# A four-layer graph network on one core: four buffers for the gathered rows instead of three

## What is computed

```python
def _genconv(h, edge_attr, src, dst, w1, b1, g1, bb1, w2, b2, t):
    msg = relu(h[src] + edge_attr) + 1e-07          # h[src]: one row per edge
    m = msg * t
    ex = exp(m - segment_max(m, dst)[dst])
    alpha = ex / (segment_sum(ex, dst)[dst] + 1e-16)
    out = h + segment_sum(msg * alpha, dst)
    z = relu(_layernorm(out @ w1 + b1, g1, bb1))
    return z @ w2 + b2
h = x @ enc_node_w + enc_node_b
e = edge_attr @ enc_edge_w + enc_edge_b
h = _genconv(h, e, ...)                             # layer 0
for i in range(1, 4):                               # layers 1 to 3
    h = h + _genconv(relu(_layernorm(h, ...)), e, ...)
return layernorm(x + relu(_layernorm(h, ...)))
```

## Time and profile before

| | us |
|---|---|
| median of 3 runs | 4429.86 |
| the three runs | 4434.78, 4423.26, 4429.86 |
| span of the profiled execution | 4412.7 |

### The profile page before, as it was taken

The page is one execution under the profiler, slowest core; times in us unless marked ns, Lnnn a source line. Parts: engine busy times, 40 slices in busy tenths (PEclk is TensorE's granted clock), DMA queues, the critical chain, the costliest instruction groups (busy, mean ns, idle before and its releaser), DMA issues.

```text
span 4412.7 us, 44760 instructions
## 1 busy us (share of the span) xinstructions
PE 2914.6 (66%) x16648; PEld 1382.9 (31%) x16648; DVE 2824.3 (64%) x2795; ACT 1741.2 (39%) x2192; POOL 2517.9 (57%) x2621
## 2 busy tenths in 40 slices
PE   3667677775437776777435777777742777777764
PEld 2223233332313333333222333333331333333333
DVE  6467678778436665666753666665763565666675
ACT  3356555545223333333432333333432333433343
POOL 6565656564366665666445666665627565655642
PEclk6778788877568888888656888887855787888875
DMA  6677778877237777777534777777734677777761
GB/s 153 162 219 204 215 195 222 219 198 174 59 100 204 204 204 192 204 204 204 133 81 115 204 204 204 205 205 201 191 76 104 160 199 199 204 202 190 211 153 40
DMA packets 1041338, 774.25 MB, mean 175 GB/s; under 512 B 914394, under 2 KB 935391, under 8 KB 1017504
## 3 DMA queue, kind: packets, MB, share of 16 engines
q1 hardware_dynamic: 934256, 446.17, 42.9%
q10 hardware_dynamic: 22048, 226.63, 14.0%
q0 software_dynamic: 84816, 98.59, 9.9%
HBM read 478.68 MB, written 292.44 MB: 175 GB/s over the span
## 4 chain that ended last, share of the span: by engine, by line
PE 41%; issue 23%; DVE 11%; ACT 10%; another core or an unknown queue 10%; POOL 4%; DMA 1%; SPq 0%; ACTq 0%; POOLq 0%; DVEq 0%
PE X L537 32%; PE X L520 5%; POOL gath L479 4%; DVE decay L885 3%; PE X L547 2%; DVE state_all L916 2%; ACT msg L647 2%; DVE X L890 1%; ACT shared L676 1%; ACT X L649 1%; ACT decay L659 1%; ACT X L664 1%; DVE state_all L900 1%; ACT decay L637 1%
## 5 line engine op out<-in xcount | busy, mean ns | idle before, releaser
L479 POOL DMA_INDIRECT gath<-z_table,idx x2488 | 2396.0, 963 | 1606.0 <-issue 750.5
L537 PE MATMUL X<-one_hot,z_parts 128*64 128x512 fp8e5 x13800 | 2103.0, 427 | 840.8 <-issue 773.1
L537 PEld LDWEIGHTS X<-one_hot,z_parts 128*64 128x64 bf16 x13800 | 939.4, 120 | 2071.2 <-issue 1542.8
L883 DVE TENSOR_TENSOR decay<-decay,top 128x1 f32<-128x1 f32 x216 | 34.2, 158 | 1358.5 <-ACT X L649 1179.6
L647 ACT ACTIVATE msg<-X,edge_bias 128x1024 f32<-128x1024 f32 (+2 forms) x216 | 228.2, 1057 | 1622.5 <-remote 1080.3
L520 PE MATMUL X<-attr,enc_edge 128*128 128x512 f32 x824 | 469.3, 688 | 221.9 <-issue 115.8
L659 ACT ACTIVATE decay<-X 128x1024 f32<-128x1024 f32 (+2 forms) x216 | 209.3, 969 | 791.7 <-DVE X L890 556.1
L871 DVE STREAM_TRANSPOSE rows_all<-state_all 128x1024 f32<-128x1024 f32 (+3 forms) x432 | 505.9, 1171 | 7.5
L885 DVE TENSOR_TENSOR_SCAN decay<-X,decay 128x1023 f32<-128x1023 f32 (+2 forms) x216 | 477.2, 2209 | 7.7
L900 DVE TENSOR_TENSOR_SCAN state_all<-decay,state_all,X 128x1024 f32<-128x1024 f32 (+2 forms) x216 | 468.2, 2167 | 20.0 <-ACT X L664 16.0
L916 DVE TENSOR_TENSOR_SCAN state_all<-decay,state_all,X 128x1024 f32<-128x1024 f32 (+2 forms) x216 | 468.0, 2167 | 0.0
(11 more groups left out here) (155 smaller groups left out, 1182.3 us busy)
## 6 DMA issues: line engine op xcount, KB each, us to landing
rows_table<-rows_all SPq DMA_DIRECT2D x784, 256.0 KB
one_hot<-one_hot_dram ACTq DMA_DIRECT2D x69, 1920.0 KB
attr<-attr_t SPq DMA_DIRECT2D x196, 512.0 KB
one_hot<-one_hot_dram ACTq DMA_DIRECT2D x69, 1280.0 KB
one_hot_dram<-one_hot SPq DMA_DIRECT2D x23, 1920.0 KB
gath<-z_table,idx POOLq DMA_INDIRECT x2488
one_hot_dram<-one_hot SPq DMA_DIRECT2D x23, 1280.0 KB
keep<-keep_dram SPq DMA_DIRECT2D x192, 128.0 KB
```

Of the source, the lines that this page charges most:

```text
L479: pool.indirect_dma_start(out=gath[s][:, n * F:(n + 1) * F], out_offset=None, in_=z_table, in_offset=bass.IndirectOffsetOnAxis(ap=idx[:, c ...
L537: last = nc.tensor.matmul(x[h * F:(h + 1) * F, BANK:CH], z_parts[:, i * GB + k, third, :], one_hot[:, i, k, h * BANK:(h + 1) * BANK], star ...
```

## The change

`gath` has four buffers and four semaphores instead of three; the other buffers keep three. POOL waits before chunk g for `x_ready` of chunk g - 4. The totals that PE waits for are counted per buffer of four. No instruction is added or taken away on PE, DVE, ACT or SP, and none changes its place: in POOL's row of instructions the wait for `x_ready` of each chunk is for one chunk earlier, and the first in layer 0 stands before chunk 4 instead of chunk 3.

```diff
 SLOTS = 3
+GSLOTS = 4
...
-    GATHERS_UP_TO.append((GATHERS_UP_TO[_g - SLOTS] if _g >= SLOTS else 0) + HALVES * (gathered_tiles(_g // NCH, _c) - first_tile(_c)))
+    GATHERS_UP_TO.append((GATHERS_UP_TO[_g - GSLOTS] if _g >= GSLOTS else 0) + HALVES * (gathered_tiles(_g // NCH, _c) - first_tile(_c)))
...
-        gath = slots("gath", SLOTS, [P, KT * HALVES * F])
+        gath = slots("gath", GSLOTS, [P, KT * HALVES * F])
...
-        attr_landed, gathered, stored = sems("attr_landed", SLOTS), sems("gathered", SLOTS), sems("stored", 2)
+        attr_landed, gathered, stored = sems("attr_landed", SLOTS), sems("gathered", GSLOTS), sems("stored", 2)
...
-                    s = g % SLOTS
-                    if g >= SLOTS:
-                        pool.wait_ge(x_ready, g - SLOTS + 1)
+                    s = g % GSLOTS
+                    if g >= GSLOTS:
+                        pool.wait_ge(x_ready, g - GSLOTS + 1)
...
             def add_rows(layer, c):
                 g = layer * NCH + c
-                s = g % SLOTS
+                s = g % GSLOTS
                 pe.wait_ge(gathered[s], 16 * GATHERS_UP_TO[g])
```

## The result

The changed kernel takes 4612.80 us (median of 4 runs, 4605.57 to 4632.76), the kernel before 4432.32 (4 runs, 4423.26 to 4436.77): ratio 1.041, interval 1.038 to 1.045. Forecast were 4510 us, range 4350 to 4640. The sign and the range held; the rise is 180 us instead of 84. The profiled execution has a span of 4603.6 us, 190.9 more than the one before.

A forecast was written before the change was run, and what follows sets the result against it. The prediction took PE's slow completions during POOL's runs of gathers, until they land, to set each section's length. Terms +40 + 66 - 22 + 0 gave +84 us on the 4429.9 us median, rounded to 4510 us; range 4350 to 4640.

The forecast's parts named there:

- the term of layer 0: Layer 0, where POOL also waits for ACT's key counts: taken as 0, bounds -45 to +80 us.
- What bounds it: PE's completions turn slow some microseconds into a run of gathers and come free when it has landed; mean pair 36.3 us.
- flip of the phase: Steady pairs: long gather moves beside the part of 90, short beside 60; long message-row intervals become odd to even.
- Beginnings: Start of each of four layers: chunk 6's gathers follow at once, releasing the part of 60 10 us later; +40 us.
- the first slow phase: First part of 60 in a layer: slow phase ends near 62 us after its start instead of 52.
- Steady pairs: 22 pairs in each of layers 1 to 3: matmuls left over behind the long gather, 1.0 us a pair, +66 us.
- meeting gathers: Six pairs in layers 1 to 3 where long and short gathers meet: half vanish, -22 us, bounds -44 and 0.
- No change: Rival: gathers only come earlier, PE's slow phases are its own and merely coincide; 4430 us, chance 0.15.
- the part of 60 slips through: Rival: part of 60 beside the short gather signals before slowness begins, section 10.0 instead of 12.1; 4331 us, chance 0.15.
- the missing buffer: Rival: POOL's pauses in each pair vanish and the pair falls to POOL's 30.0 us; 4014 us, chance 0.05.
- Gathers meet in every pair: Rival: long gather follows short without pause, +7.3 us a pair, some 4950 us; half the pairs or more, chance 0.13.
- The estimate from the queue of 64: PE beyond a stuck matmul: 32 matmuls at most taken in, part of 90 caught sooner than 60; left out of sum.

The follow-up runs named there:

- held4: Changed kernel (four buffers) plus a PE wait: transposes of chunk c wait until the gathers of chunk c + 3 have landed; 5023.00 us, ratio 1.144.
- layer0_third: Changed kernel, but in layer 0 POOL waits for x_ready of chunk g - 3 as before; 4433.41 us beside 4403.39 for the kernel before, ratio 1.006.
- place A: Name for the four experiment groups in which the unchanged kernel before took about 3567 us; the changed kernel's ratios there were 0.9999, 1.0002 and 1.0003.
- place B: Name for groups in which the unchanged kernel before took about 4400 us (4395.66 and 4403.39), the first measurement being of this kind; changed kernel there 1.041.

## Why the prediction was right in sign and too small

The step that failed is the term of layer 0, which the prediction put at nothing: it measured +80.8 us. A second term, the section from row 3 to row 4 (+32.1 us), was missing. The others came out near their values, the steady pairs by luck.

- **What bounds it, right.** POOL's gathers, the landing and PE's slow phases in lock-step. The flip of the phase with four buffers and the flip back with five show it, which no busy share says.
- **Beginnings, +40: right.** Measured +45.3 (11.7, 10.9, 10.9, 11.8), and the first slow phase took the 62 us that the prediction named. But the term was not whole: the interval from row 3 to 4 grew too, +32.1 in layers 1 to 3, since chunk 7's long gather now lies in it, and at the layer's end the rows 44 to 48 gave back 36.2. The prediction had neither; they nearly cancel, and held4 shows both without the rest.
- **Steady pairs, +66 and meeting gathers -22, sum +44: mechanism right, the sum met by luck.** Over the prediction's own 22 pairs, rows 4 to 48, layers 1 to 3 took +40.9 us. But that is +77.1 in the first twenty and -36.2 in the last two, where the gathers beside them get shorter. Matmuls are left over behind the long gather's landing, as said: the median lag of the message row grew from 3.4 us to between 5.6 and 5.9. The median pair grew from between 36.2 and 36.9 us to 38.1, so by 1.2 to 1.9: inside the bounds of 0 to 2.1, above the 1.0 taken. Pairs over 41 us fell only from six to four. Nor is the size steady: in the group of layer0_third the same program had lags of 4.2 to 5.1 us, and its twenty pairs +0.5 us in three layers. Why is open.
- **Layer 0, 0: this is the step that failed.** Measured +80.8, of which 11.7 is the start; with the old wait in layer 0 alone it is -5.6. The text saw that "the fourth buffer is held back by the next wait in the same row" and that the gathers of two chunks would meet more often; it then took 0 from between -45 and +80 because "no row is nearer". There was one: the intervals of ACT's message rows in layer 0, 26.4 and 16.2 us, of which the 16.2 are ACT's own work. It says that a short gather that leaves its place there is added in full, 10.1 us a pair, and that the key gather behind it can't come before those 16.2 us are over. With some eight pairs that is +80 and not a middle value. This is worked out afterwards; measured are +76 over nine pairs (rows 5 to 23), four of them at 10.0 to 11.5 us.
- Put together, with the prediction's own 22 pairs: 191 = 84 + 69 (layer 0 beyond its start) + 32 (row 3 to row 4 in layers 1 to 3) + 5 (starts) - 3 (the pairs) and 4 us of small differences elsewhere.
- **The rivals.** "No change" and "the part of 60 slips through" were wrong in the first measurement (the short interval is 12.7 us, not 10.0), and no change is what place A showed, for a reason that the prediction didn't have: PE has no slow phases there. Wrong was also the missing buffer, which the Trainium skill's rule on repeating gaps (Perfetto Trace Analysis, Optimization Strategy) stood beside: the gap before the long gather stayed at 2.7 us and the one before the short gather grew from 3.8 to 6.6 (medians of layer 2), with one buffer more. So the gap was no missing buffer. The rule speaks of the engine that should be saturated, and POOL, busy for 57%, was not that engine in the first measurement: the trace doesn't contradict the rule, its condition wasn't met. "Gathers meet in every pair" is what happened in layer 0, up to chunk 23, at 8.5 us a pair in the mean.
- **The burst.** In the changed kernel's row PE takes in 66 of the 90 matmuls at speed, for 8 us into the long gather; where before 12 were through when the long gather had landed: part and gather now begin together. The estimate from the queue of 64 (TensorE: Matmul & The Clock Gate, of the Trainium skill) wasn't needed, and no run here tests it further.

## What to carry to other kernels

A buffer more on an engine that isn't late lets its work start earlier, and so beside other work: ask for each stage of the program what lies beside that work now, what it slows there, and which wait is next in the same row. Where two streams go in lock-step, a longer distance between them moves work from the end of a loop to its start; here the two nearly cancelled, and the cost was in what no longer overlapped. And where a term's bounds are as wide as the whole forecast, look for the row that decides it before taking a middle.

## What the runs showed of the hardware

The same kernel took 3567 to 3571 us in four groups and 4396 to 4432 in the other two and the first measurement, 23 to 24% more, while the runs of the kernel before in one group lie within about 1%. POOL's cost of a gather (966 and 967 ns) and its gap of 0.30 us were the same in both. What differed was PE: with gathers under way, at place B a part of 90 was not through before the gathers were, at place A it took 9.90 us beside them. The mean granted clock of the kernel before was 0.771 in the first measurement and 0.82 at place A; the difference of 6% can't make 24%; whether it follows from PE's pauses or not is not shown. A verdict on such a change (here 1.041 or 1.000) can depend on the group of runs, and the kernel before, run in the same group, is what makes it readable.
